# Group attentions: score matmuls of a tile in one piece, value matmuls in one piece behind the next tile's queries

## The reference

```python
def _mha(x, wqs, wks, wvs, pw, pb, g, b):          # 16 heads of 64
    q = jnp.einsum('mld,hdk->mhlk', x, wqs)
    k = jnp.einsum('mld,hdk->mhlk', x, wks)
    v = jnp.einsum('mld,hdv->mhlv', x, wvs)
    scores = jnp.einsum('mhqk,mhsk->mhqs', q, k) / jnp.sqrt(jnp.asarray(dk, x.dtype))
    attn = jax.nn.softmax(scores, axis=-1)
    out = jnp.einsum('mhqs,mhsv->mhqv', attn, v) - v
    out = out.transpose(0, 2, 1, 3).reshape(m, l, h * dv)
    out = out @ pw + pb
    return _layernorm(out + x, g, b)

def _ffn(x, w1, b1, w2, b2, g, b):
    h = jax.nn.relu(x @ w1 + b1)
    return _layernorm(h @ w2 + b2 + x, g, b)
...
x = _mha(x, la_...); x = _ffn(x, lf_...)
x = x.reshape(b, l // nl, nl, d).transpose(0, 2, 1, 3).reshape(-1, l // nl, d)
x = _mha(x, sa_...); x = _ffn(x, pf_...)
```

## Time and profile before

| | us |
|---|---|
| median of 3 runs | 2158.68 |
| lowest and highest | 2153.34, 2159.38 |
| the profiled execution, time | 2152.56 |
| the profiled execution, span | 2150.7 |
| PE busy in the span | 2013.3 (94%) |
| DVE, ACT, POOL busy | 1388.9, 1046.8, 972.7 |

### The profile page before, as it was taken

The page is one execution under the profiler, slowest core; times in us unless marked ns, Lnnn a source line. Parts: engine busy times, 40 slices in busy tenths (PEclk is TensorE's granted clock), DMA queues, the critical chain, the costliest instruction groups (busy, mean ns, idle before and its releaser), DMA issues.

```text
span 2150.7 us, 54537 instructions
## 1 busy us (share of the span) xinstructions
PE 2013.3 (94%) x22465; PEld 1685.7 (78%) x22465; DVE 1388.9 (65%) x3108; ACT 1046.8 (49%) x2108; POOL 972.7 (45%) x762
## 2 busy tenths in 40 slices
PE   6999999999999999769999779999999999989994
PEld 4777777777777776558888669999989999988883
DVE  6767666766676666347878775555566455456983
ACT  3666666666666666314545444243245234324551
POOL 1655555555555555315455352343433334344440
PEclk9999999999999999979999889999999999999996
DMA  7001020101011001211130120000121000030000
GB/s 272 9 18 55 11 101 11 55 11 57 22 44 46 13 11 42 100 61 42 48 135 11 50 74 14 22 12 13 46 75 52 17 32 17 17 124 25 11 16 15
DMA packets 59990, 97.16 MB, mean 45 GB/s; under 512 B 7720, under 2 KB 50480, under 8 KB 57392
## 3 DMA queue, kind: packets, MB, share of 16 engines
q1 hardware_dynamic: 57184, 86.69, 12.1%
q10 hardware_dynamic: 2560, 6.99, 0.8%
HBM read 70.45 MB, written 23.20 MB: 44 GB/s over the span
## 4 chain that ended last, share of the span: by engine, by line
PE 42%; DVE 7%; issue 4%; ACT 2%; POOL 2%; DVEq 0%; POOLq 0%; ACTq 0%
PE psum L262 13%; PE psum L273 10%; PE psum L1814 4%; PE psum L1802 2%; PE psum L2306 2%; PE psum L243 2%; PE psum L1788 2%; PE psum L1130 1%; PE psum L1143 1%; PE psum L222 1%; DVE b_act L1375 1%; PE psum L2340 1%; DVE b_acc L1383 1%; POOL b_act_lo L1287 1%; ACT e_pr L2445 1%
## 5 line engine op out<-in xcount | busy, mean ns | idle before, releaser
L761 POOL TENSOR_TENSOR a_sm<-a_sm,a_rsum 128x1024 f32<-128x1024 f32 x256 | 479.7, 1893 | 381.1 <-DVE a_rsum L793 379.0
L781 DVE CUSTOM_DVE_ANT_0 a_sm<-psum,a_strip 128x1024 f32<-128x1024 f32 x256 | 312.0, 1219 | 145.2 <-PE psum L621 145.2
L700 ACT ACTIVATE a_sm<-a_sm,a_mn 128x1024 f32<-128x1024 f32 x256 | 294.0, 1149 | 27.2 <-DVE a_mn L781 26.0
L634 PE MATMUL psum<-ident,a_sm 128*128 128x128 f32 x2048 | 275.8, 277 | 6.5 <-POOL a_sm L761 3.3
L705 ACT ACTIVATE a_pT<-psum 128x512 f32<-128x512 f32 x256 | 151.6, 592 | 266.8 <-PE psum L634 266.8
L634 PEld LDWEIGHTS psum<-ident,a_sm 128*128 128x128 f32 x2048 | 223.9, 141 | 65.6 <-issue 45.8
L649 PE MATMUL psum<-a_pT,a_V 128*64 128x256 f32 x2048 | 249.0, 385 | 0.6 <-ACT a_o L711 0.6
L649 PEld LDWEIGHTS psum<-a_pT,a_V 128*64 128x64 f32 x2048 | 136.2, 136 | 77.2 <-issue 22.0
L788 DVE COPY a_pT<-psum 128x512 f32<-128x512 f32 x256 | 174.9, 683 | 13.5 <-PE psum L634 8.1
L1898 ACT ACTIVATE g_val<-psum 128x512 f32<-128x512 f32 x64 | 38.1, 596 | 221.9 <-PE psum L1814 221.9
L1287 POOL TENSOR_TENSOR b_act_lo<-b_act,b_act_hi 128x512 fp32r<-128x512 f32 x64 | 91.1, 1428 | 103.9 <-ACT b_act_hi L1185 103.9
(11 more groups left out here) (329 smaller groups left out, 4232.0 us busy)
## 6 DMA issues: line engine op xcount, KB each, us to landing
a_strip<-table SPq DMA_DIRECT2D x16, 960.0 KB, 6.5
oT<-a_o SPq DMA_DIRECT2D x64, 128.0 KB, 1.9
b_oT_in<-oT SPq DMA_DIRECT2D x8, 1024.0 KB, 5.4
a_raw<-in_a_wqkv SPq DMA_DIRECT2D x7, 384.0 KB, 3.3
s_x<-in_x_rev SPq DMA_DIRECT2D x4, 512.0 KB, 7.5
vb<-s_zero SPq DMA_DIRECT2D x8, 256.0 KB, 2.7
b_x_in<-in_x SPq DMA_DIRECT2D x8, 256.0 KB, 5.6
b_vb_in<-vb SPq DMA_DIRECT2D x8, 256.0 KB, 5.4
```

The source lines that it names most:

```text
L634: last = pe.transpose(psum[:, 4 + j, k * P:(k + 1) * P], sm[:, st % RING, kt * P:(kt + 1) * P], ident[:, :])
L700: a.activation(sm[:, st % RING, :], sm[:, st % RING, :], ACT.Exp, scale=-1.0, bias=mn[:, at:at + 1], accum_out=rsum[:, at:at + 1]).then_in ...
L761: g.tensor_tensor(sm[:, st % RING, :], sm[:, st % RING, :], rsum[:, at:at + 1].broadcast_to([P, T]), ALU.mult).then_inc(sig("scaled"), 1)
L781: v.tensor_tensor_reduce(out=sm[:, st % RING, :], in0=scores_banks(hl).rearrange("p c n -> p (c n)"), in1=strip[:, pair % 2, hl, qt * P:qt ...
```

## The change

In each step both score bursts are issued together, behind the first half's values. Before, half 1's burst stood behind the second half's values and the transposes `fT`. Both bursts of value matmuls are issued together too, behind the next tile's first two query units, which stood between them. The list `units` is put in the same order, so the hand-out of the banks moves with it. ACT, DVE, POOL and SP keep their order.

```diff
@@ list of units
-        units += [("dv", 4 * s), ("dv", 4 * s + 1), ("ds", 4 * s), ("ds", 4 * s + 1), ("dv", 4 * s + 2), ("dv", 4 * s + 3)]
+        units += [("dv", 4 * s), ("dv", 4 * s + 1)] + [("ds", 4 * s + i) for i in range(4)] + [("dv", 4 * s + 2), ("dv", 4 * s + 3)]
         if back:
             units += [("fT", s - 1)]
-        units += [("ds", 4 * s + 2), ("ds", 4 * s + 3)]
         if s + 1 < NG:
             units += [("dT", s + 1)]
         if back:
             units += [("f1", 4 * (s - 1) + i) for i in range(4)]
-        units += [("do", 4 * s + i) for i in range(4)]
         if s + 1 < NG:
             units += [("dq", 4 * s + 4), ("dq", 4 * s + 5)]
+        units += [("do", 4 * s + i) for i in range(4)]
@@ tensor
                 scores(s, 0)
+                scores(s, 1)
                 own_values(s, 1)
             if back:
                 pe.wait_ge(sig("a1"), s)
                 part_columns(pe, sig, banks, "fT", s - 1, z, ident)
-            if front:
-                scores(s, 1)
             if s + 1 < NG:
                 columns(pe, s + 1)
@@
             if front:
-                values(s, 0)
                 if s + 1 < NG:
                     queries(pe, s + 1, (0, 1))
+                values(s, 0)
                 values(s, 1)
```

## The result

The changed kernel is slower, by far more than predicted: **2279.36 us** median of four runs (2278.31 to 2280.39) against 2159.03 us before, a ratio of **1.056** (95% interval 1.053 to 1.058). The forecast was 2167.6 us, at most 2179. The profiled execution has a span of 2276.4 us against 2150.7: 125.7 us more.

A forecast was written before the change was run, and what follows sets the result against it. PE's own matmul stream was taken to bound steps 1 to 14. The terms 12.2 (14 steps) - 1.3 (step 0) + 0.7 (step 15) made +11.6 us, added to the runs' mean of 2156.0: 2167.6 us, range 2157 to 2179.

The forecast's parts named there:

- What bounds the kernel, and the ways a change of order can act: Steps 1 to 14: PE's matmul stream, busy 576.05 of 580 us; reordering gains only between pieces, loses at early waits.
- The sum of a step: Steps 1 to 14: f1 1.09 us later, value side gives back 0.22; net 0.87 us slower a step, +12.2 us.
- The prediction's last sign of being wrong: Steps 1 to 14: a granted clock below 1.00 beyond the one place would show the prediction wrong.
- step 15: Last step, no dT behind fT: new stall partly replaces its 1.07 us gap; +0.2 to +1.2 us, +0.7 taken.
- The gaps of 1.88 us and 1.07 us: PE standing before the change: 1.88 us in step 7, slower clock behind; 1.07 us in step 15, usual pace behind.
- The stall ahead of f1: Between dT and f1 each middle step: PE waits 1.24 us for g_zT's low part, its 1.25 us cover gone.
- The seams: Entering and leaving bursts: joining saves 0.22 us a step for values, 0.15 for scores, 0.37 together.
- Step 0: First step, 4.56 us gap: queries go into its end; -1.3 us taken, nothing to -4 us possible.
- Rival 1: The new stall trips the clock in a third of the steps: 8.5 us on top, 2176 us; chance 0.13.
- Rivals 2 and 3: Rival 2: seams worth 0.74 us a step, 2162 us, chance 0.17; rival 3: f1 doesn't stall, 2149.5 us, chance 0.08.

## Why the prediction was wrong

- **What bounds the kernel, and the ways a change of order can act.** This step failed. It said that a change of PE's order can gain only at seams and lose only at waits for other engines. There is a third: how fast the instructions themselves are used up. The sum of a step had the two joined bursts without any gap. They held 62.7 us of gaps, and with those right behind them the gaps that no engine ended rose from 6.0 to 65.4 us; through the clock came most of another 48. The prediction's last sign of being wrong, a granted clock below 1.00 in the middle steps, came true.
- **The trace of before had it.** The prediction took the joined value bursts of step 15 as proof that joining saves 0.04 us, and stopped reading at their end. The rows that follow show PE standing twice:

```profile
1910.57 0.62 PE L273 MATMUL psum<-g_w,g_h 128*128 128x256 f32 x3 [0.76 <-DVE g_h L2076]
1911.93 5.42 PE L273 MATMUL psum<-g_w,g_h 128*128 128x256 f32 x45 [0.74 <-issue]
```

  The 0.74 us that no engine ended, three matmuls behind the only burst of 512 instructions in that kernel, was the supply gap: it ends 1.47 us after a packet's landing. The wait for g_h just ahead of it had probably hidden a part. The gaps of 1.88 us and 1.07 us also followed a burst or stood in one. The prediction used them for the clock and for step 15, and did not ask what made them.
- **The stall ahead of f1.** Right. The chain of 2.06 us from fT to f1 was 2.06 us; the gap, 1.24 by the prediction, reads 1.02 in the profile, which counts dT to the modelled end of its last transpose; 15 steps of it make 15.6 us.
- **The seams.** Right as far as they can be seen: from f1 to the queries 5.79 us (5.76 expected), from the queries to the bursts 2.97 (2.96).
- **Step 0.** Sign wrong. The queries did go into the gap, which fell from 4.56 to 2.62 us, but the scores and the values held gaps of their own, 2.91 and 2.16 us, with slow pieces around them. From the first values to the second queries it took 27.0 us instead of 21.5, where 1.3 less were expected.
- **Rival 1, the clock.** The right behaviour from the wrong cause. It was weighed for a stall of 1.24 us, in a third of the steps, at 8.5 us. The bf16 kernel with the joined scores has that stall in every step and keeps 0.99, so it costs no clock. The gaps of about 2 us in and behind the bursts do: behind 24 of the 29 gaps of over 1.5 us the clock fell to the 1.2 GHz level, behind five of 1.55 to 2.16 us it did not. They are as long as the 1.88 us after which the clock fell before.
- **Rivals 2 and 3** played no part.

What stays open: how the 48 us split between the gaps' length and the light work around them, why five long gaps left the clock up, and why blocks come 4 us apart in the bursts although a packet takes 1.3 us.

## What to carry to other kernels

Count a burst of small instructions in instructions, not in time: over 200 a microsecond outran the supply here as soon as two blocks of 256 were used up in a row, while 256 between two large pieces hardly ever did (7 gaps in the whole stage before). Before joining small pieces, read what the trace has behind its longest burst, and take a gap ended by "issue" as a sign, not as noise. And when a piece moves, look at what it covered: the 1.25 us of score matmuls between fT and f1 were worth their place, and so was their length.

## What the runs showed of the hardware

PE's program came in packets of 16 KB, 256 instructions, on a queue of its own. With over 200 small instructions a microsecond, PE stopped at the second block edge in a burst, for 1.5 to 2.5 us in 27 of the 29 long gaps (2.9 and 5.1 us in the others), at a place that could be told to one matmul from the count of instructions in a step. It went on 1.2 to 1.6 us after a packet had landed. Behind most such gaps the granted clock dropped (0.67 over the 9 us around one), so that a gap of 2.35 us cost another 2.5 us in the twelve matmuls behind it. A gap of 1.03 us in every step, ended by DVE, left the clock at 0.99.
